# First attention of a two-layer block on raw transposed rows, with the layer norm's scale applied to the scores on VectorE

## The reference, cut to what matters

```python
x = x + tanh(g_xattn[0]) * L0_xattn(layernorm(x), ctx, ctx)   # one head, 77 keys, width 256
x = x + tanh(g_ffn[0])   * L0_ffn(layernorm(x))               # 256 -> 1024 -> 256, quantised piecewise GELU
x = x + tanh(g_xattn[1]) * L1_xattn(layernorm(x), ctx, ctx)   # 16 heads
x = x + tanh(g_ffn[1])   * L1_ffn(layernorm(x))               # top 2 of 8 experts, 512 slots each
# L0_xattn: softmax((xn @ Wq + bq) @ (ctx @ Wk + bk).T) @ (ctx @ Wv + bv)
```

## Time and profile before

| what | us |
|---|---|
| runs before, median (lowest to highest) | 492.54 (491.83 to 492.64) |
| the profiled execution | 491.95 |
| its span, first to last instruction | 490.2 |
| PE busy | 454.8 (93%) |
| PEld busy | 395.9 (81%) |
| DVE busy | 370.4 (76%) |
| ACT busy | 258.6 (53%) |
| POOL busy | 145.6 (30%) |

### The profile page before, as it was taken

How to read it: one execution, slowest core, us unless ns; L and a number is a source line. 1 busy time by engine, 2 the same in 40 slices (tenths; PEclk the granted TensorE clock), 3 DMA queues, 4 the chain that set the end, 5 groups by cost and what they waited for, 6 DMA issues and landing times.

```text
span 490.2 us, 8549 instructions
## 1 busy us (share of the span) xinstructions
PE 454.8 (93%) x3226; PEld 395.9 (81%) x3226; DVE 370.4 (76%) x753; ACT 258.6 (53%) x416; POOL 145.6 (30%) x122
## 2 busy tenths in 40 slices
PE   6999999999998999998997499999999999999991
PEld 4787789798887888787886259989999999999991
DVE  4689998898988978899898966686757475757441
ACT  2577899697965664556554132463434344442220
POOL 3354100010002211222113063215263645445153
PEclk9999999999999999999999799999999999999997
DMA  7412200000000101312123341134363747461031
GB/s 243 136 43 60 82 1 2 0 1 1 1 0 1 45 1 44 117 57 87 45 86 127 126 125 55 23 130 136 98 162 96 170 96 195 86 174 20 3 48 16
DMA packets 37135, 36.06 MB, mean 74 GB/s; under 512 B 6442, under 2 KB 35942, under 8 KB 36966
## 3 DMA queue, kind: packets, MB, share of 16 engines
q1 hardware_dynamic: 30633, 27.65, 17.3%
q0 software_dynamic: 6144, 7.66, 9.1%
q10 hardware_dynamic: 317, 0.21, 0.1%
HBM read 27.69 MB, written 8.39 MB: 74 GB/s over the span
## 4 chain that ended last, share of the span: by engine, by line
PE 75%; DVE 15%; issue 4%; DMA 2%; ACT 1%; POOL 1%; ACTq 0%; DVEq 0%; POOLq 0%
PE PS L1489 19%; PE PS L1490 18%; PE PS L1491 18%; PE PS L1898 5%; PE PS L1509 2%; DVE nmaxC L1181 2%; PE PS L1844 2%; PE PS L1909 2%; DVE xn L1020 1%; DVE tmp L1184 1%; DVE st L993 1%; DMA tmp<-in_L_xattn_Wk 1%; PE PS L1546 1%; PE PS L1760 1%; DVE tmp L1231 1%
## 5 line engine op out<-in xcount | busy, mean ns | idle before, releaser
L1489 PE MATMUL PS<-w_hi,hT_hi 128*128 128x256 f32 x384 | 110.3, 287 | 0.8 <-DVE hT_lo L1161 0.6
L1490 PE MATMUL PS<-w_lo,hT_hi 128*128 128x256 f32 x384 | 108.6, 283 | 0.0
L1491 PE MATMUL PS<-w_hi,hT_lo 128*128 128x256 f32 x384 | 108.6, 283 | 0.0
L964 ACT ACTIVATE tmp<-PS,biasT 128x512 f32<-128x512 f32 (+1 forms) x80 | 43.8, 600 | 111.1 <-PE PS L1491 111.1
L673 POOL DMA_INDIRECT out<-tmp,dst_idx x32 | 56.1, 1754 | 98.6 <-DVE tmp L1445 91.8
L1489 PE MATMUL PS<-xT_hi,w_hi 128*128 128x512 f32 (+1 forms) x224 | 81.6, 364 | 1.1 <-DVE xT_lo L1028 1.1
L1490 PE MATMUL PS<-xT_lo,w_hi 128*128 128x512 f32 (+1 forms) x224 | 80.8, 361 | 0.0
L1491 PE MATMUL PS<-xT_hi,w_lo 128*128 128x512 f32 (+1 forms) x224 | 80.4, 359 | 0.0
L1489 PEld LDWEIGHTS PS<-w_hi,hT_hi 128*128 128x128 f32 x384 | 73.4, 191 | 4.1 <-issue 2.2
L1490 PEld LDWEIGHTS PS<-w_lo,hT_hi 128*128 128x128 f32 x384 | 73.5, 191 | 0.8
L1491 PEld LDWEIGHTS PS<-w_hi,hT_lo 128*128 128x128 f32 x384 | 73.5, 191 | 0.0
(11 more groups left out here) (254 smaller groups left out, 819.9 us busy)
## 6 DMA issues: line engine op xcount, KB each, us to landing
w_raw<-in_L_ffn_w SPq DMA_DIRECT2D x72, 256.0 KB, 3.0
residual<-in_x SPq DMA_DIRECT2D x4, 512.0 KB, 5.3
out<-residual SPq DMA_DIRECT2D x3, 512.0 KB, 4.2
normed_rows<-xn SPq DMA_DIRECT2D x3, 512.0 KB, 3.6
kv<-in_L_ffn_b SPq DMA_DIRECT2D x1, 1024.0 KB, 6.5
tmp<-in_L_xattn_Wq SPq DMA_DIRECT2D x2, 256.0 KB, 5.4
out<-residual SPq DMA_DIRECT2D x2, 256.0 KB, 4.2
normed_rows<-xn SPq DMA_DIRECT2D x2, 256.0 KB, 3.1
```

Of the source, the lines that this page charges most:

```text
L964: act.activation(gD[:, G % 2, f, 0:P * n], H[:, G % 2, f, 0:P * n], ACT.Gelu, bias=biasT[:, col:col + 1]).then_inc(e_gelu, 1)
L1489: pe.matmul(o, lh, rh, start=start, stop=False, skip_group_check=skip)
L1490: pe.matmul(o, lh, rl, start=False, stop=False, skip_group_check=skip)
L1491: return pe.matmul(o, ll, rh, start=False, stop=stop, skip_group_check=skip)
```

## The change

The first attention no longer normalises its rows. The host lays out x transposed beside x, the context transposed, Wq and the second attention's Wo transposed, and all biases as columns; SP loads each chunk of x twice, as rows and as columns (`xT_raw`). DVE takes the mean out of Wq's columns (`centre_queries`), so that the raw rows times KW need only the row's `rstd` as a factor. `attend_scores` is eight products on raw columns, without a wait on the norm; DVE's `largest(c)` then multiplies each tile of scores by `rstd`, adds the bias row `beta` and writes it to SBUF (`sA`), and takes the largest. Rounds 0 to 3 have statistics and a power, but no apply, transposes or copy.

The scores of chunk 0 stand on PE in front of the second attention's keys (`keys(5, wk1_sb)`) and the two value products. Rounds 4 and 5 of the feed-forward are applied by ACT instead of DVE. The split of the second attention's Wq moves from DVE to ACT (rounded part) and POOL (rest). `high_parts` of units 2 and 3 move into step 0 of the feed-forward on ACT, with `apply(5)` between them. Wo's transposes on PE and their copy on ACT go; its transpose is loaded. `stats_to` maps a round to its place in the new order of statistics (0, 1, 2, 4, 3, 5, ...).

The core of the diff, by engine (declarations of semaphores and tiles, and index changes that follow from the fewer rounds, are left out):

```diff
@@ SP @@
-            load_x(0)
-            sp.dma_start(wq0_sb, Wq0.rearrange("(k p) e -> p k e", p=P)).then_inc(wq0_loaded, 16)
-            load_x(1)
...
+                sp.dma_start(xT_raw(c), xT.rearrange("(k p) n -> p k n", p=P)[:, :, 512 * c:512 * c + 512]).then_inc(xT_loaded[c], 16)
+
+            sp.dma_start(wk0_sb, Wk0).then_inc(ctx_loaded, 16)
+            sp.dma_start(wqT, WqT0.rearrange("(k p) d -> p k d", p=P)).then_inc(wq0_loaded, 16)
+            for c in range(NC):
+                load_x(c)
...
+            sp.wait_ge(a_scores, 3)
             for dst, src in ((wo[:, :, 0:D], Wo1.rearrange("(k p) e -> p k e", p=P)),
+                             (woT, WoT1.rearrange("(a p) r -> p a r", p=P)),
@@ POOL @@
             power(0)
+            pool.memset(Vblk[:, :, :, 0:P], 0.0).then_inc(vblk_zeroed, 1)
             power(1)
-            pool.wait_ge(xn_ready, 2)
-            pool.memset(Vblk[:, :, :, 0:P], 0.0).then_inc(vblk_zeroed, 1)
             power(2)
-            for c in range(1, NC):
-                pool.wait_ge(a_scores, c + 1)
-                low_parts(c - 1, 0, 1)
-                power(c + 2)
-                low_parts(c - 1, 1, 2)
-            pool.wait_ge(knot_ready, 1)
-            low_parts(NC - 1)
+            power(NC)
+            low_parts(0, 0, 1)
+            power(3)
+            low_parts(0, 1, 2)
+            pool.wait_ge(wq_rounded, 1)
+            pool.tensor_tensor(wq_lo[:, :, :], wq1_raw, wq_hi[:, :, :].bitcast(F32), ALU.subtract).then_inc(wq_split, 1)
+            low_parts(1)
+            power(NC + 1)
+            low_parts(2)
+            low_parts(3)
             power(NC + 2)
@@ ACT @@
-            for c in range(NC):
-                exponentials(c)
-                if c + 1 < NC:
-                    x_copy(c + 1)
-                else:
-                    x_hi(NC)
-                    act.activation(small[:, 20:21], small[:, 16:17], ACT.Gelu)
-                if c == 0:
-                    first_values()
-                act.wait_ge(a_tr, c + 1)
-                act.activation(eAT[0:KEYS, :], ATA[c % 2][0:KEYS, :], ACT.Copy).then_inc(a_trcopied, 1)
-                if c == 0:
-                    second_keys()
-                high_parts(c)
...
+            act.activation(KW, PS[:, 6, 0:KD * 2 * KEYS].rearrange("p (m b k) -> p m b k", m=KD, b=2),
+                           ACT.Copy).then_inc(kw_copied, 1)
...
+            act.wait_ge(v0_psum, 1)
+            act.wait_ge(tanh_ready, 1)
+            act.activation(V0[0:KEYS, :, :], PS[0:KEYS, 0, :].rearrange("p (b d) -> p b d", b=2), ACT.Copy,
+                           scale=tg[0:KEYS, 0:1]).then_inc(v0_copied, 1)
...
+            exponentials(0)
+            copy_turned(0)
+            exponentials(1)
+            copy_turned(1)
+            exponentials(2)
+            copy_turned(2)
+            high_parts(0)
+            act.wait_ge(query_loaded, 32)
+            act.activation(wq_hi[:, :, :], wq1_raw, ACT.Copy).then_inc(wq_rounded, 1)
+            apply(NC)
+            x_hi(NC)
+            exponentials(3)
+            act.activation(small[:, 20:21], small[:, 16:17], ACT.Gelu)
+            high_parts(1)
+            copy_turned(3)
+            act.wait_ge(wq_split, 1)
...
                     if g + 1 < NB_PAIRS:
                         to_grid(g + 1)
+                    if g == 0:
+                        high_parts(PAIRS - 2)
+                        apply(NC + 1)
+                        high_parts(PAIRS - 1)
@@ DVE @@
+            centre_queries()
...
+                for i in range(4):
+                    dve.scalar_tensor_tensor(out=sA[:, c % 2, i, :], in0=SA[c % 2][:, i, :], scalar=rstd[:, c, i:i + 1],
+                                             in1=beta[:, c // (NC // 2), :], op0=ALU.mult, op1=ALU.add).then_inc(a_shift, 1)
+                dve.wait_ge(a_shift, 4 * (c + 1))
+                dve.tensor_reduce(soft[:, c % 2, 0, :], sA[:, c % 2, :, :], AX_X, ALU.max, negate=True).then_inc(a_max, 1)
...
+            largest(0)
+            stats(1)
+            invert(0)
+            stats(2)
+            largest(1)
+            attended(0)
+            largest(2)
+            stats(NC)
+            invert(1)
+            attended(1)
+            shifts(NC, 1)
+            stats(3)
+            invert(2)
+            attended(2)
             x_lo(NC)
-            attended(NC - 2)
-            apply(NC + 1)
+            largest(3)
+            stats(NC + 1)
+            invert(3)
+            shifts(NC + 1, 1)
             dve.wait_ge(tanh_ready, 1)
             output_units()
@@ PE @@
-                pe.matmul(SA_pad[c % 2], ones_hl, bcast(bq_pad[:, b, :].unsqueeze(1), [33, 4, KP]),
-                          start=True, stop=False, skip_group_check=True)
...
+                        ins = pe.matmul(SA[c % 2][:, i, :], xT_raw(c)[:, k, P * i:P * i + P],
+                                        KW[:, k, b, :], start=(k == 0), stop=(k == KD - 1))
...
-            for c in range(1, NC):
-                attend_scores(c)
-                transpose_x(c + 1)
-                attend_values(c - 1)
-                attend_turn(c)
+            attend_turn(0)
+            attend_scores(1)
+            attend_values(0)
+            attend_scores(2)
+            attend_turn(1)
+            attend_values(1)
+            attend_turn(2)
+            attend_scores(3)
+            attend_values(2)
+            transpose_x(NC)
+            attend_turn(3)
```

More of the change, by code:

```diff
@@ L169, in flamingo_gated_two_layers @@
         ctxT = take(0, 2, KEYS)
-        xT_odd = take(1, KD, 512)
+        xT_third = take(1, KD, 512)
         V1 = take(1, 2, D)
-        eA = take(1, 4, KEYS)
+        sA = take(1, 2, 4, KEYS)
+        beta = take(1, 2, KEYS)
         KW = take(1, KD, 2, KEYS)
-        wv1_sb = take(1, D)
-        bv0_row = take(1, D)
+        wv1_sb = take(0, D)
+        bv0_row = take(0, D)
         bo_row = bo_bc[:, 0:D]
@@ L257, in flamingo_gated_two_layers @@
         O = PS[:, 6:8, :].rearrange("p b (t d) -> p (b t) d", d=D)
-        SA_pad = [PS[:, 2 + 2 * i, 0:4 * KP].rearrange("p (t n) -> p t n", t=4) for i in range(2)]
-        SA = [s[:, :, 0:KEYS] for s in SA_pad]
+        SA = [PS[:, 2 + 2 * i, 0:4 * KEYS].rearrange("p (t n) -> p t n", t=4) for i in range(2)]
         ATA = [PS[:, 3 + 2 * i, :] for i in range(2)]
@@ L277, in flamingo_gated_two_layers @@
         wq0_loaded = sem("wq0_loaded")
-        b0_loaded = sem("b0_loaded")
+        bias_loaded = sem("bias_loaded")
+        xT_loaded = [sem(f"xT_loaded{c}") for c in range(NC)]
+        wq_centred = sem("wq_centred")
+        keys_psum = sem("keys_psum")
+        kw_psum = sem("kw_psum")
+        v0_psum = sem("v0_psum")
+        a_shift = sem("a_shift")
+        wq_rounded = sem("wq_rounded")
+        wq_split = sem("wq_split")
         v0_loaded = sem("v0_loaded")
@@ L755, in _ @@
-            act.wait_ge(v1_psum, 1)
-            act.activation(V1[0:KEYS, :, :], PS[0:KEYS, 7, :].rearrange("p (b d) -> p b d", b=2),
-                           ACT.Copy).then_inc(v1_copied, 1)
-            def exponentials(c):
-                act.wait_ge(a_max, c + 1)
-                if c >= 1:
-                    act.wait_ge(a_tr, c)
-                for i in range(4):
-                    act.activation(eA[:, i, :], SA[c % 2][:, i, :], ACT.Exp, bias=soft[:, c % 2, 0, i:i + 1],
-                                   accum_out=soft[:, c % 2, 1, i:i + 1]).then_inc(a_exp, 1)
@@ new lines, in _ @@
+            act.wait_ge(bias_loaded, 16)
+            act.wait_ge(keys_psum, 1)
+            for m in range(KD):
+                ins = act.activation(KT0[:, m, :], PS[:, 4, m * 2 * KEYS:(m + 1) * 2 * KEYS], ACT.Identity,
+                                     bias=biasT[:, BK0 + m:BK0 + m + 1])
+            ins.then_inc(kt_copied, 1)
+            act.wait_ge(kw_psum, 1)
+            act.activation(beta, PS[:, 3, 0:2 * KEYS].rearrange("p (b k) -> p b k", b=2), ACT.Copy).then_inc(kw_copied, 1)
+            act.wait_ge(kw_psum, 2)
@@ new lines, in _ @@
+            link(ins)
+            act.wait_ge(keys_psum, 2)
+            for m in range(KD):
+                for h in range(2):
+                    act.activation(Kpar[:, m, :, h, :], PS[:, 5, m * 2 * KEYS:(m + 1) * 2 * KEYS]
+                                   .rearrange("p (b k) -> p b k", b=2), ACT.Identity, scale=par[:, h:h + 1],
+                                   bias=parbk[:, h, m:m + 1]).then_inc(keys_placed, 1)
+            act.wait_ge(v0_loaded, 16 * N_V0)
+            act.activation(tg[:, :], gates[:, :], ACT.Tanh).then_inc(tanh_ready, 1)
@@ L1551, in _ @@
             keep_warm(4, 6)
-            pe.wait_ge(ctx_loaded, 16 * N_CTX)
-            for b in range(2):
-                ins = pe.transpose(PS[:, 2, KEYS * b:KEYS * (b + 1)], ctx_sb[0:KEYS, b, :], ident[0:KEYS, 0:KEYS])
-            ins.then_inc(setup_psum, 1)
             def keys(bank, w):
@@ L1633, in output_bias @@
                 for k in range(KD):
```

(17 more changed lines are left out.)

283 lines of the change are left out of this document (101 added, 182 removed).

## The result

The changed kernel takes 511.06 us (median; 508.45 to 511.51) against 492.27 us for the kernel before on the same chip: a ratio of 1.0369, 95% interval 1.0346 to 1.0392. The direction was forecast, the size was not: 498.9 was the forecast and 503.0 the end of its range. The traced execution took 510.95 us with a span of 509.2, so 19.0 us more span than before. Eight experiments (e1, e2, g3, g5, g6, h1, h2, k1) have one run more than 1.5% above their fastest, which the medians take in and every ratio but e1's leaves out; in h1, h2 and k1 it is the traced one, whose trace serves only to show what TensorE did.

The account below looks back on a forecast made before the run. TensorE fills the first feed-forward from 60 us, so a late opening reaches the end. Second round's transposes at 54.6 instead of 48.74 (+5.9), Wo's transposes gone (-0.45), slow restart (+1.5): +6.95, 498.9 us, range 494.8 to 503.

Parts of the forecast that it names:

- Part 1: Up to the attention's first scores: they start at 11.8 us instead of 16.08, 4.3 us earlier.
- s: Start time of the attention's first scores on TensorE: 11.3 or 12.3 us by KW's pace, taken as 11.8.
- Part 2: From first scores to the attention's last exponentials: 27.6 us instead of 22.9.
- largest(3): VectorE's scaling and maximum of the last chunk's scores, ahead of exponentials(3): 1.4 us, bounds 1.0 and 2.1.
- Part 3: From the last exponentials to the second round's transposes: one line across four queues, 15.2 us instead of 9.8.
- part 4: Behind the second round's transposes: Wo's four transposes go, minus 0.45 us; slow clock after TensorE's idling, plus 1.5.
- rival (b): The clock falls in the attention too, ahead of turn(0), costing up to 5 us more: about 504; chance 0.11.
- the pause of the earlier trace: TensorE's 5.53 us idling before 279.53 in the old profile; half pace for 3.7 us afterwards, losing 1.9.
- (a): Rival: the clock costs nothing, neither at first scores nor at a restart; plus 4.95 us, 496.9; chance 0.24.
- (c): Rival: faster, the waits ahead of the second round's transposes run side by side; 487.3 us; chance 0.07.
- (d): Rival: gain and loss cancel over the kernel, within 0.2% (1 us); chance 0.04.
- (e): Rival: the doubled load of x brings chunk 3's columns two or three us late; 501.5 us; chance 0.04.

Follow-up runs that it names:

- e1: Changed kernel with nine fill products (about 2 us) put into TensorE's idle stretch ahead of turn(0); 500.2 us, ratio 1.0203.
- e2: As e1, with 24 fill products ahead of turn(3) and 30 ahead of the second round's transposes as well; 500.6 us, ratio 1.0158.
- g3: Changed kernel with e1's nine fill products and GpSimd's power of round 5 ahead of unit 1's low parts; 500.1 us, ratio 1.0134.
- g5: Changed kernel with the forecast's waits loosened, ScalarE's weight work spread over its idle time in the attention, round 5 normalised on ScalarE; 493.45 us, ratio 1.0039.
- g6: As g5, with unit 2's high parts on ScalarE behind round 5's normalisation; 492.51 us, ratio 1.0009.
- h1: Changed kernel with g2's copy order, round 5 normalised on VectorE again and unit 2's high parts moved forward on ScalarE; 497.23 us, ratio 1.0106.
- h2: Changed kernel with exactly the four fill products back ahead of turn(0) that the change removed; 499.17 us, ratio 1.0136.
- k1: Kernel before the change, without the four fill products ahead of turn(0) and with V0 copied ahead of exponentials(0); 499.14 us, ratio 1.0132.
- e3: Changed kernel with GpSimd's power of round 5 ahead of unit 1's low parts, no fill; 510.46 us, ratio 1.0399.
- g2: Changed kernel without fill, with the copies of V1 and V0 on ScalarE moved behind exponentials(0); 497.92 us, ratio 1.0117.
- g1: Kernel before the change with only the four fill products (0.86 us) ahead of turn(0) taken out; 492.3 us, ratio 0.9993.

## Why the prediction was wrong

**Right.** Part 1: first scores at 11.30 (11.3 to 12.3), but the number is luck. The transfer of chunk 0's columns released them, which part 1 did not count, and not KW's copy, which had ended at 10.28. Where the columns came in time, s was 10.43 (e1), 0.9 under the lower bound, or 12.02 (e2): KW's eight products (L1570) took 1.06 us in the one and 2.07 in the other. By the rule that the Trainium skill gives on its page "TensorE: Matmul & The Clock Gate", section on the PE-mode transpose, KW was to run at the upper rate once the early transposes were gone. The runs do not settle it: of the twelve traces without these transposes five (e2, e3, g2, g3, h2) have KW at half pace, and k1, which has the transposes, had the first eight of L1509 done in 1.09 us, where the kernel before took 1.92 (1.71 in the chain of the earlier trace rows). Part 2's chain: exponentials(0) stand behind V0's copy, and with the clock up (e1) the stretch is 27.55 us (27.6). largest(3), bounded at 1.0 and 2.1 and taken as 1.4, is 0.91 + 0.48 = 1.39. Part 3: with the clock up (e1) 14.4 us (15.2), through the Gelu table, unit 1's high and low parts, the power, the look-ups, the grid and apply(5), in that order; g3 shows that the low parts in front of the power weigh 0.9 us in it and not 2.4, because the grid comes last as soon as they are gone. In the changed kernel itself 14.6 us is near the forecast by luck: there TensorE, with ten of hidden(0)'s twelve products at half pace, ended hidden(1) at 60.45, and the forecast's own line (the look-ups, L848, end at 60.35) came 0.1 us before it.

**The step that failed** is in part 4 and rival (b). The clock's price was put at one slow restart, 1.5 us, behind the second round's transposes; its fall in the attention was rival (b), with a chance of 0.11 and "up to 5 more". It happened, in the trace and, to judge by the times (none under 508.45) and the mean clocks (0.942 to 0.951), in every timed run of the changed kernel, and cost 11.2 us in the attention: 38.8 against 27.6. Two things were wrong. The argument against it, that gaps were under 1 us otherwise, looked at the other gaps, where the one of 2.1 us was enough (e1, g2 and k1 show it). And the price counted scores, three products and a turn, as though the clock would come back with steady work, as it does behind the pause of the earlier trace rows. It did not come back in 36 us, of which TensorE worked from 18.9 to 44.9 with under 1 us of pauses. What this attention's products show is lopsided: they kept the upper rate where they found it (e1, and g2 without any fill) and did not bring it back where they found the lower (the changed kernel, k1, h1, and h2 by its durations).

**The sum, corrected.** Forecast +6.95 us. Part 2 was 11.2 longer, s 0.5 and part 3 0.6 shorter. From the transposes to the next fill the changed kernel takes 5.65 us against 3.61, 2.0 more (forecast 1.5). The transposes come 16.0 later (forecast 5.9), that fill 18.0 (70.35 against 52.35). Behind the four transposes of Wo, which are gone, the lateness is 17.5, so they take off about the 0.45 that was forecast, and it stays at 17.5 up to the products at 279.53, which the changed kernel starts at 296.96. By the first products of L1940 (L1918 in the changed kernel) it is 19.1. Before, then after:

```profile
301.77 1.57 PE L1940 MATMUL PS<-tmp 128*128 128x96 bf16 x32
```

```profile
320.83 1.56 PE L1918 MATMUL PS<-tmp 128*128 128x96 bf16 x32
```

That last 1.6 us arises in a stage that the change leaves as it was: between these two starts lie 22.2 us before, 23.9 in the changed kernel, and 24.9 in g1, whose code there is that of the kernel before. So it need not come of the change, since the same code varies by more; why it varies no run shows.

**The rivals.** (a), the clock costs nothing, is near what g2 and e2 come to, 497.9 and 500.6 against its 496.9. g2 still has the later falls (0.50 in 36 to 42 us); e2, with its fill, has a clock of 1.00 to past 72 us. So with the fall in the attention away, the change still makes the kernel slower by 1.2 to 1.6%. (c) fails on parts 2 and 3, (d) on the size. (e): chunk 0's columns were what the first scores waited for, 1.49 us, but TensorE never waited for a later chunk's.

## What to carry to other kernels

Before you take work off TensorE, ask what its next instruction will wait for: a pause of 2 us in front of cheap products cost 11 here. Price a fall of the clock as half pace for everything up to the next stage that has been seen to lift it, not as one restart. And look for the order that closes the pause before you look for fill: two small copies moved behind the exponentials gave back 13 us, with no product added, where nine fill products gave back 11.

## What the runs showed of the hardware that was not expected

The granted-clock column can miss a slow array: in h2 it says 1.00 from 10 to 50 us while products of one shape take 3.66 us instead of the 1.98 of e1. Durations of a known product are the surer sign.

VectorE and GpSimd hold each other up. In the changed kernel, VectorE and then GpSimd in order of time:

```profile
63.64 3.27 DVE L1142 SCALAR_TENSOR_TENSOR tmp<-tmp 128x1024 f32<-128x1024 uint16 x1
...
73.92 1.23 DVE L1142 SCALAR_TENSOR_TENSOR tmp<-tmp 128x1024 f32<-128x1024 uint16 x1
```

```profile
52.59 2.36 POOL L586 TENSOR_TENSOR w_lo<-w_raw,w_hi 128x1024 fp32r<-128x1024 f32 x1 [9.73 <-ACT w_hi L708]
...
62.76 6.38 POOL L586 TENSOR_TENSOR w_lo<-w_raw,w_hi 128x1024 fp32r<-128x1024 f32 x2 [6.84 <-ACT w_hi L708]
```

The same instruction (L1142) takes 3.27 us beside GpSimd's low parts and 1.23 without them; GpSimd's two take 6.38 where one alone takes 2.36. Both of VectorE's inputs to L1142 and to the shifts lie in SBUF, the on-chip memory that GpSimd's low parts read as well. The Trainium skill, page "SBUF — State Buffer", section "Who interferes with whom", says that a VectorE instruction with two SBUF inputs contends with a GpSimd instruction that reads SBUF. The trace agrees, with those numbers. g5's shifts show that even an instruction of 4 columns can be held up: 2.35 us, to within 0.02 us of the end of the low parts beside it, against 0.16 in g6.
